# Inverting the 16x16 diagonal blocks of a triangle on GpSimd instead of four doubling levels on TensorE

## What is computed

```python
def step(S, inp):
    qt, kt, vt, gt, bt = inp
    S = S * jnp.exp(gt)[..., None, None]
    mem = jnp.einsum('bhk,bhkv->bhv', kt, S)
    delta = (vt - mem) * bt[..., None]
    S = S + jnp.einsum('bhk,bhv->bhkv', kt, delta)
    o = jnp.einsum('bhk,bhkv->bhv', qt * scale, S)
    return (S, o)
```

## Time and profile before

| | |
|---|---|
| median of 3 runs | 3080.88 us (3077.23 to 3086.05) |
| span of the profiled execution | 3086.7 us |
| TensorE busy | 2650.6 us, 86% |
| VectorE busy | 2285.6 us, 74% |
| ScalarE busy | 1761.1 us, 57% |
| GpSimd busy | 591.9 us, 19% |
| mean granted TensorE clock | 0.926 of full |
| delta_rule's first and last gains power on GpSimd (63 turns between) | 150.5 and 2586.4 us |

### The profile page before, as it was taken

One profiled execution on the slowest core, in us unless ns is written; L12 is line 12 of the kernel. 1 busy time (PEld: TensorE's weight loads), 2 busy tenths in 40 slices (PEclk: granted clock), 3 DMA queues, 4 the chain that ended last, 5 costly groups with the idle time before them and its releaser, 6 DMA issues. The chain is left out here.

```text
span 3086.7 us, 71844 instructions
## 1 busy us (share of the span) xinstructions
PE 2650.6 (86%) x22496; PEld 2187.0 (71%) x22496; DVE 2285.6 (74%) x5647; ACT 1761.1 (57%) x4019; POOL 591.9 (19%) x733
## 2 busy tenths in 40 slices
PE   1389899999898898898898898898898899587887
PEld 0268778788787787787787787787787787354455
DVE  4479888798797797888888797798897798133434
ACT  1157666676676676676676676676676677211121
POOL 0022222222222222222222122222222222000000
PEclk6699999999999999999999999999999999798888
DMA  2301020001000100010001000100010000200000
GB/s 83 97 25 38 2 65 19 21 14 53 26 25 14 53 25 26 14 53 26 26 14 53 26 25 14 53 25 26 14 53 26 26 14 1 83 1 28 27 27 7
DMA packets 93598, 96.20 MB, mean 31 GB/s; under 512 B 31217, under 2 KB 82106, under 8 KB 93250
## 3 DMA queue, kind: packets, MB, share of 16 engines
q1 hardware_dynamic: 93250, 91.44, 9.8%
HBM read 72.10 MB, written 2.54 MB: 24 GB/s over the span
## 5 line engine op out<-in xcount | busy, mean ns | idle before, releaser
L716 DVE TENSOR_TENSOR dr_w<-dr_ps,mask 128x512 bf16<-128x512 f32 x768 | 523.2, 681 | 170.5 <-PE dr_ps L526 167.6
L730 DVE SCALAR_TENSOR_TENSOR dr_y<-dr_ps,dr_cw,dr_y 128x255 f32<-128x255 f32 (+2 forms) x1344 | 574.6, 475 | 29.1 <-ACT dr_y L855 22.5
L848 ACT CAST dr_tt<-dr_ps 128x512 bf16<-128x512 f32 x768 | 460.4, 600 | 1.2 <-PE dr_ps L546 1.2
L845 ACT CAST dr_tn<-dr_ps 128x512 bf16<-128x512 f32 x640 | 374.9, 586 | 147.6 <-PE dr_ps L539 147.6
L630 PE MATMUL dr_ps<-dr_w,dr_am 128*128 128x96 f32 x3072 | 421.9, 281 | 2.5 <-ACT dr_w L907 2.5
L630 PEld LDWEIGHTS dr_ps<-dr_w,dr_am 128*128 128x128 f32 x3072 | 382.8, 194 | 11.0 <-ACT dr_w L907 3.0
L546 PE MATMUL dr_ps<-dr_tt,dr_w 128*128 128x128 bf16 x3072 | 297.7, 219 | 74.6 <-DVE dr_w L716 74.6
L552 PE MATMUL dr_ps<-dr_hb,dr_wqk 128*128 128x256 f32 x1024 | 287.7, 430 | 23.7 <-DMA dr_hb<-hT 22.7
L526 PE MATMUL dr_ps<-dr_tn,dr_b 128*128 128x128 bf16 x3072 | 297.1, 219 | 0.0
L539 PEld LDWEIGHTS dr_ps<-dr_w,dr_tt 128*128 128x128 bf16 x2560 | 186.4, 98 | 141.5 <-issue 70.4
L907 ACT COPY dr_w<-dr_ps 128x384 f32<-128x384 f32 x384 | 188.8, 492 | 134.2 <-PE dr_ps L630 134.0
(11 more groups left out here) (187 smaller groups left out, 4843.6 us busy)
## 6 DMA issues: line engine op xcount, KB each, us to landing
dr_abc<-scr_a SPq DMA_DIRECT2D x64, 512.0 KB, 3.9
dr_hb<-hT SPq DMA_DIRECT2D x64, 256.0 KB, 2.5
dr_bcb<-scr_b SPq DMA_DIRECT2D x128, 64.0 KB, 3.2
ex_modb<-scr_mod SPq DMA_DIRECT2D x4, 1024.0 KB, 6.7
dr_wo<-in_Wo SPq DMA_DIRECT2D x1, 3072.0 KB, 11.3
dr_wv<-in_Wv SPq DMA_DIRECT2D x8, 384.0 KB, 4.0
dr_wg<-in_Wg SPq DMA_DIRECT2D x8, 384.0 KB, 3.9
p_x<-in_x SPq DMA_DIRECT2D x4, 512.0 KB, 6.2
```

What stands on the lines that cost most here:

```text
L716: v.tensor_tensor((tn if l == 0 else w16)[:, us, :], ps[:, (X0, X1)[g], :].rearrange("p (u n) -> p u n", u=QH), bc(mask[:, l, :], 1, QH), ...
L730: v.scalar_tensor_tensor(y[:, slot, x:T], ps[:, (A0, A1)[n % 2], off:off + T - x], cw[:, t, TAPS - 1 - x:TAPS - x], y[:, slot, x:T], ALU.m ...
L845: act.copy(tn[:, us, :], ps[:, (X2, X1)[g], :].rearrange("p (u n) -> p u n", u=QH)).then_inc(s["tn_ok"], 1)
L848: act.copy(dst, ps[:, (X0, X2)[g], :].rearrange("p (u n) -> p u n", u=QH)).then_inc(s["tt_ok"], 1)
```

## The change

The levels of block size 1, 2, 4 and 8 are no longer done on TensorE. The eight 16x16 blocks on the diagonal of each of the 8 triangles of a step are inverted by substitution on GpSimd, and only the last three levels (block sizes 16, 32, 64) remain (`LEVELS = 3`, `LVL0 = 4`). They stand in halves 8 to 14; halves 0 to 7 have no merges.

For a substitution along the free axis each partition needs its whole 16x16 block, so the blocks are spread by DMA through DRAM. New on SP, once a step:

```diff
+            def blocks(it):
+                m = it % NB
+                wait_apart(sp, s["b16_ok"], (it + 1) * CH, s["passed_sp"])
+                wait_apart(sp, s["ab_ld"], it * (16 * NB16), s["passed_sp"])
+                for n in range(NB16):
+                    rows = slice(n * BASE, (n + 1) * BASE)
+                    sp.dma_start(scr["d"][n], b16[rows, m, :, rows]).then_inc(s["d_st"], 16)
+                wait_apart(sp, s["d_st"], (it + 1) * (16 * NB16), s["passed_sp"])
+                wait_apart(sp, s["xb_ok"], it, s["passed_sp"])
+                for n in range(NB16):
+                    sp.dma_start(ab[n * BASE:(n + 1) * BASE].rearrange("p j u i -> p (j u i)"),
+                                 scr["d"][n].rearrange("j u i -> (j u i)").partition_broadcast(BASE)
+                                 ).then_inc(s["ab_ld"], 16)
```

A store takes 16 rows, 8 triangles and 16 columns (128 runs of 32 bytes, 4 KB); a load gives 16 partitions the same 4 KB. On GpSimd (`B_AT`: half 5, 6 and 7 hold j = 0 to 4, 5 to 9 and 10 to 14):

```diff
+            def base(st, part):
+                it, m = st
+                n = it * (2 * BASE - 2)
+                if part == 0:
+                    wait_apart(pool, s["ab_ld"], (it + 1) * (16 * NB16), s["passed_pool"])
+                    wait_apart(pool, s["c32_ok"], it, s["passed_pool"])
+                    pool.tensor_copy(xb[:], bc(const[:, C_E16:C_E16 + BASE], 1, U)).then_inc(s["xs"], 1)
+                for j in range(SPLIT[part], SPLIT[part + 1]):
+                    left = BASE - 1 - j
+                    wait_apart(pool, s["xs"], n + 2 * j + 1, s["passed_pool"])
+                    pool.tensor_tensor(xt[:, :, 0:left], bc(xb[:, :, j], 2, left), ab[:, j, :, j + 1:BASE],
+                                       ALU.mult).then_inc(s["xs"], 1)
+                    wait_apart(pool, s["xs"], n + 2 * j + 2, s["passed_pool"])
+                    ins = pool.tensor_tensor(xb[:, :, j + 1:BASE], xb[:, :, j + 1:BASE], xt[:, :, 0:left], ALU.add)
+                    ins.then_inc(s["xb_ok"] if j == BASE - 2 else s["xs"], 1)
```

On VectorE, in half 7 ahead of stage a's `gains` and `taps`, the blocks are laid out as `tt` and, transposed, as `tn`, with zeros elsewhere (`bd32` is a bf16 mask of 32x32 blocks):

```diff
+            def expand(st):
+                it, m = st
+                v.wait_ge(s["xb_ok"], it + 1)
+                v.tensor_tensor(c32[:].rearrange("p u (h i) -> p u h i", h=2), bc(xb[:], 2, 2),
+                                bc(const[:, C_HALF:C_HALF + 2 * BASE].rearrange("p (h i) -> p h i", h=2), 1, U),
+                                ALU.mult).then_inc(s["c32_ok"], 1)
+                v.wait_ge(s["c32_ok"], it + 1)
+                v.transpose(c32t[:].rearrange("p u i -> p (u i)"), c32[:].rearrange("p u i -> p (u i)")
+                            ).then_inc(s["c32t_ok"], 1)
+                wait(v, s["p3"], it * LEVELS * 2)
+                blk = bc(bd32[:].rearrange("p (n i) -> p n i", i=2 * BASE), 1, U)
+                v.tensor_tensor(tt[:].rearrange("p u (n i) -> p u n i", i=2 * BASE), bc(c32[:], 2, P // (2 * BASE)), blk,
+                                ALU.mult).then_inc(s["te_ok"], 1)
+                v.wait_ge(s["c32t_ok"], it + 1)
+                v.tensor_tensor(tn[:].rearrange("p u (n i) -> p u n i", i=2 * BASE), bc(c32t[:], 2, P // (2 * BASE)), blk,
+                                ALU.mult).then_inc(s["te_ok"], 1)
```

TensorE's first product of the remaining levels waits for both:

```diff
                 if l == 0:
-                    pe.wait_ge(s["b16_ok"], it * CH + g + 1)
+                    pe.wait_ge(s["te_ok"], (it + 1) * 2)
...
-            for half in range(2 * LEVELS + 1):
-                if b and half:
-                    on["merge2"](b, (half - 1) // 2, (half - 1) % 2)
-                if b and half < 2 * LEVELS:
-                    on["merge1"](b, half // 2, half % 2)
-                for st, pieces in ((a, A_FIRST), (c, C_AT), (d, D_AT), (a, A_AT)):
+            for half in range(HALVES):
+                k = half - M_FIRST
+                if b and k > 0:
+                    on["merge2"](b, (k - 1) // 2, (k - 1) % 2)
+                if b and 0 <= k < 2 * LEVELS:
+                    on["merge1"](b, k // 2, k % 2)
+                for st, pieces in ((a, A_FIRST), (c, C_AT), (b, B_AT), (d, D_AT), (a, A_AT)):
```

More of the change, by code:

```diff
@@ L28 @@
 U = CH * QH
-LEVELS = 7
+BASE = 16
+NB16 = P // BASE
+LEVELS = 3
+LVL0 = 4
+SPLIT = (0, 5, 10, BASE - 1)
 REFINE = 2
@@ L388, in delta_rule @@
             kqb_ok r_ok r16_ok p1 p2 p3 mask_ok tn_ok tt_ok
+            d_st ab_ld xs xb_ok c32_ok c32t_ok te_ok
             w0_ps res_ps d_ps s_ps ks_ps o_ps ot_ps wo_ps w_ok rs_ok S_ok r1_ok r1h_ok sqo_ok mso_ok vo_ok fo_ok
@@ L973, in scale @@
                 pool.tensor_tensor(fo[:], vo[:], nhalf[:], ALU.pow).then_inc(s["fo_ok"], 1)
-            on.update(qk_silu=squares, gains=gains, negate=select, mean=scale)
+            def base(st, part):
[13 more added lines that the diff above has]
+                    ins.then_inc(s["xb_ok"] if j == BASE - 2 else s["xs"], 1)
+            on.update(qk_silu=squares, base=base, gains=gains, negate=select, mean=scale)
             pool.memset(half[:], 0.5).then_inc(s["set_ok"], 1)
```

60 lines of the change are left out of this document (42 added, 18 removed).

## The result

The changed kernel takes 3865.8 us (median of 4 runs, 3863.4 to 3869.2) against 3083.5 us for the kernel before in the same comparison: 1.254 times the time (95% interval 1.252 to 1.256). The forecast was 3815 us, the range 3400 to 4300.

The account below looks back on a forecast made before the run. TensorE bounds the kernel before; after the change a closed chain does: 12.7 + 15.5 + 3.5 + 18.5 = 50.2 us a turn against 38.7, times 64, giving 3815 us, range 3400 to 4300.

Parts of the forecast that it names:

- a chain through a turn: Round trip, substitution, expansion and gains-to-select follow one another, so a turn takes at least their sum, 50.2 us against 38.7.
- X: The substitution on GpSimd, one copy and 30 small dependent operations: 15.5 us a turn, bounds 8.6 to 24.
- Rival (a): The chain is hidden behind TensorE's other work and the kernel gets faster, 2767 us if TensorE is the bound; chance 4%.
- Y: Round trip of the blocks through DRAM, eight stores, a wait, eight loads: 12.7 us a turn, bounds 10.1 to 18.8.
- E: The expansion on VectorE, four operations after the substitution: 3.5 us a turn, or 2.3 if all-bf16 products run twice as fast.
- (b): Rival: cheap GpSimd hops of 0.1 us and DMA issues of 0.45 us, slower by far less, 3356 us; chance 18%.
- (c): Rival: small GpSimd operations cost a power's fixed part, substitution 24 us, 4361 us in all; chance 17%.
- the hop: Wait between dependent GpSimd operations of the substitution: 0.23 us each, 6.9 us for 30.
- the signs named: Expected profile signs, among them eight stores started within 4 to 5 us, first load some 6 us after the second select.
- The power: The `mean(0)` power on GpSimd, between the substitution's first and second part: 1.2 us with its hop.
- M: Stretch from the gains on VectorE to the second select that finishes the next B: 18.5 us, bounds 17.5 and 20.
- The jump: TensorE's pause where the main loop jumps back, 8.3 us, was to be covered by its wait for the chain.

Follow-up runs that it names:

- e5: Changed kernel with the substitution's copy and 30 small operations on VectorE, directly ahead of the expansion, instead of on GpSimd: 3374.9 us.
- e4: Changed kernel without the substitution's thirty products and sums on GpSimd; DMAs, copy and expansion stay: 2802.7 us.
- e7: Changed kernel with six turns instead of three in the main loop's body, so it jumps back 10 times instead of 20: 3896.4 us.
- e10: Changed kernel with five steps in flight, expansion and merges a turn later, the substitution's last six columns behind the next turn's squares: 2846.9 us.

## Why the prediction was right, point by point

**The mechanism.** Its main step, that the change closes a chain through a turn and that TensorE's saved time becomes waiting, is what the runs show: taking 7.7 us from X took 7.7 us from the turn with the other terms in place (e5), and taking nearly all of X left a turn of 34.1 us in which the landing, the copy and the expansion still let each other go (e4). Rival (a) falls since Y, X and E came to 31.1 us, not under 20.2; (b) and (c) fall by the hop and the fixed cost below.

**Y**, 12.7 forecast, 13.1 measured. The stores started 0.74 us apart, not 0.6, near the 0.76 of the earlier trace rows; 7 of them make 1.0 us more, and the first store came 0.4 us behind the select, not 0.2. The landing was shorter than taken for the loads: from the start of the last issue to the copy it is 2.4 us, not 3.2. Loads were issued 0.45 us apart, as forecast. Of the signs named, the stores missed theirs (started within 5.2 us, not 4 to 5; first load 7.6 us behind the select, not 6).

**X**, 15.5 forecast, 16.0 measured, and that it came so close is in part luck, for two of its errors nearly cancel. The hop on GpSimd's own semaphore is 0.18 us, not 0.23: 5.4 instead of 6.9 us. The fixed part of a small operation is not the memset's 0.104: 8 elements took 0.22 us and 120 took 0.40 to 0.44, so 0.21 us fixed and 1.6 ns an element. The 30 operations are busy 9.3 us where I had 3.8 + 3.1 = 6.9. So +2.4 us against -1.5. The power cost 0.8, not 1.2.

**E**, 3.5 forecast, 2.0 measured. The large products took 0.65 and 0.68 us for 1024 elements, where a product of 512 f32 elements takes 0.692. Of the two prices that the prediction left side by side the lower one was right. By the rule of the Trainium skill ("VectorE: DVE Perf Modes", section "What auto-detection actually checks") they were to take some 0.68 us, an estimate; the trace agrees. The wake of 0.2 us was not to be seen either (0.03 us from the last sum to the expansion), so that E lies under its lower price of 2.3, too.

**M**, 18.5 forecast, 20.1 measured in the turn shown and 19.85 in the mean, at its upper bound of 20. I had set one missing group of merges (0.7 us less) against the clock (1.5 us more) and called it even. e4 has M at 18.5 with the clock at 1.00, so nothing is to be seen of the missing merges, and the clock cost 1.6 us. In the kernel after, four gate instructions behind the pause took 2.77 us (1.46 us in the same place of e4, at 1.00), and the first eight of line 669 1.97 us (1.13 us).

**The jump.** The prediction had the pause covered by the wait. It is not covered, it isn't there: TensorE has no wait for issue at the jump in the kernel after; the one that VectorE has instead is covered, by the round trip. Where TensorE's pause is back (e7), the program is 30.6 us slower, through Y: that a covered pause costs nothing is not what that run shows. And the 33.8 us for a turn bound by TensorE, and with it the 2767 us of rival (a), was worked out with the pauses inside and is no lower bound: TensorE is busy 30.3 us of a turn at full clock (e4, e10), and turns of e10 without a jump take 32.9.

**The sum.** 64 x (50.8 - 38.7) = 774 us, and the spans differ by 3865.0 - 3086.7 = 778 us. The forecast of 3815 us lies 51 us under the measured time. That this is so little is in part luck as well: in the turn shown the terms were off by +0.4, +0.5, -1.5 and +1.6 us, and E's error makes up for nearly all of M's.
